# Level totals, query copies and small products of an RWKV time-mix and feed-forward kernel, in another order and form

## The reference

```python
xx  = x_prev - x
mix = tanh((x + xx * time_maa_x) @ maa_w1).reshape(b, t, 5, 32)
mw, mk, mv, mr, mg = einsum('btfe,fec->fbtc', mix, maa_w2)
r, k, v = (x + xx * (maa_r + mr)) @ Wr.T, ...          # one form for each
g = silu((x + xx * (maa_g + mg)) @ Wg.T)
w = time_decay + tanh((x + xx * (maa_w + mw)) @ td_w1) @ td_w2
decay = exp(-exp(w))
# per head of 32 channels, token after token:
y = r @ (S + u * k v^T);   S = decay * S + k v^T
x = layernorm(x + (groupnorm(y) * ln_g + ln_b) * g @ Wo.T)
h = layernorm(gelu(x @ sign(W_fc)^T)) ;  x = layernorm(x + h @ sign(W_proj)^T)
```

## Time and profile before

| what | value |
|---|---|
| median of 3 runs | 3308.46 us (3307.17 to 3309.01) |
| the profiled execution | 3307.6 us |
| its span, first to last instruction | 3305.7 us |
| PE busy | 3080.0 us, 93% |
| DVE busy | 2449.2 us, 74% |
| ACT busy | 1913.6 us, 58% |
| POOL busy | 933.9 us, 28% |
| mean granted TensorE clock | 0.982 |

### The profile page before, as it was taken

One profiled execution on the slowest core, in us unless ns is written; L12 is line 12 of the kernel. 1 busy time (PEld: TensorE's weight loads), 2 busy tenths in 40 slices (PEclk: granted clock), 3 DMA queues, 4 the chain that ended last, 5 costly groups with the idle time before them and its releaser, 6 DMA issues.

```text
span 3305.7 us, 98915 instructions
## 1 busy us (share of the span) xinstructions
PE 3080.0 (93%) x39133; PEld 2229.9 (67%) x39133; DVE 2449.2 (74%) x5172; ACT 1913.6 (58%) x3919; POOL 933.9 (28%) x825
## 2 busy tenths in 40 slices
PE   1899999999999999999999999999999999999997
PEld 0667666767666767666767666767666767666765
DVE  8467787777787777787777687777777777787777
ACT  0456566556566556566655566655566655566654
POOL 3223322223322223322233322233322233322232
PEclk9899999999999999999999999999999999999999
DMA  5000000000000000000000000000000000000000
GB/s 198 14 8 21 15 18 21 18 14 21 15 18 21 18 14 21 16 17 21 18 14 21 20 13 21 18 15 20 21 12 21 18 16 19 21 12 21 18 21 14
DMA packets 22741, 73.24 MB, mean 22 GB/s; under 512 B 3088, under 2 KB 3344, under 8 KB 20688
## 3 DMA queue, kind: packets, MB, share of 16 engines
q1 hardware_dynamic: 22352, 66.96, 5.9%
HBM read 50.17 MB, written 16.78 MB: 20 GB/s over the span
## 4 chain that ended last, share of the span: by engine, by line
PE 48%; DVE 27%; ACT 13%; issue 10%; DVEq 1%; DMA 1%; ACTq 0%; POOL 0%; SPq 0%; POOLq 0%
PE psP L393 10%; PE psP L425 7%; PE psF L637 5%; PE psP L591 5%; ACT HHI L820 4%; PE psF L618 4%; DVE HLO L1288 4%; ACT ARENA L661 3%; DVE ARENA L1138 3%; ACT GG L811 2%; DVE SUMS L1280 2%; DVE ARENA L1126 2%; PE psW L464 2%; PE psW L481 2%; DVE ARENA L1169 2%
## 5 line engine op out<-in xcount | busy, mean ns | idle before, releaser
L661 ACT ACTIVATE ARENA<-ARENA 32x512 f32<-32x512 f32 (+3 forms) x1026 | 581.1, 569 | 263.9 <-DVE ARENA L1114 202.1
L393 PE MATMUL psP<-ARENA,WALL 128*128 128x256 f32 x3072 | 688.0, 380 | 0.2 <-ACT ARENA L694 0.2
L393 PEld LDWEIGHTS psP<-ARENA,WALL 128*128 128x128 f32 x3072 | 574.4, 190 | 73.7 <-issue 0.7
L1288 DVE SCALAR_TENSOR_TENSOR HLO<-GG,FWB,HHI 128x128 f16<-128x128 f32 x1024 | 302.0, 357 | 368.1 <-ACT HHI L820 362.9
L618 PE MATMUL psF<-XHI,WFC 128*128 128x128 f16 x4096 | 487.0, 220 | 2.4 <-DVE ST L1306 2.1
L618 PE MATMUL psF<-XLO,WFC 128*128 128x128 f16 x4096 | 485.7, 219 | 0.0
L618 PEld LDWEIGHTS psF<-XHI,WFC 128*128 128x128 f16 x4096 | 400.4, 99 | 31.5 <-issue 26.3
L881 POOL TENSOR_TENSOR ARENA<-ARENA,XT 128x1024 f32<-128x1024 f32 x128 | 278.2, 2174 | 505.5 <-DVE ARENA L1059 505.5
L618 PEld LDWEIGHTS psF<-XLO,WFC 128*128 128x128 f16 x4096 | 401.4, 98 | 17.6 <-issue 10.3
L637 PE MATMUL psF<-WPJ,HHI 128*128 128x512 f16 x1024 | 405.7, 396 | 4.7 <-ACT GG L811 4.7
L637 PE MATMUL psF<-WPJ,HLO 128*128 128x512 f16 x1024 | 402.3, 393 | 0.0
(11 more groups left out here) (164 smaller groups left out, 5298.9 us busy)
## 6 DMA issues: line engine op xcount, KB each, us to landing
XT<-x_ch SPq DMA_DIRECT2D x33, 520.0 KB, 3.4
ARENA<-x_tok SPq DMA_DIRECT2D x32, 512.0 KB, 4.8
out<-OUT SPq DMA_DIRECT2D x64, 256.0 KB, 3.0
WALL<-w_all SPq DMA_DIRECT2D x5, 1024.0 KB, 15.9
ARENA<-wfc SPq DMA_DIRECT2D x4, 1024.0 KB, 8.0
ARENA<-wpj SPq DMA_DIRECT2D x3, 1024.0 KB, 14.8
GG<-wpj SPq DMA_DIRECT2D x1, 1024.0 KB, 18.8
OUT<-w2a SPq DMA_DIRECT2D x8, 64.0 KB, 15.2
```

Source lines behind the costliest of these rows:

```text
L393: mm = pe.matmul(psP[:, P.bank(f"{name}{g}"), COLS * c:COLS * (c + 1)], WALL[:, w, k, 128 * (2 * g + c):128 * (2 * g + c + 1)], cc(XF[slot ...
L661: return act.activation(o, i, ACT.Copy)
L1288: e = dve.scalar_tensor_tensor(out=HLO[:, k, :], in0=GG[:, u % 2, 0, 128 * m:128 * (m + 1)], scalar=FWB[:, 0, k:k + 1], in1=HHI[:, k, :], ...
```

## The change

**Totals first.** VectorE forms all six totals in one run (`totals`), behind the second quarter's sums and ahead of the u products. Before, each total followed its level's `scale_left`.

**Queries a level ahead.** In step i of the levels, VectorE scales the right halves of the next level first (`scale_right(i + 2, 2 * n)`), then the left halves of the present one, and then makes its own copy of the next level's queries. ScalarE's copies wait for `r_scaled` as before, which now comes a level sooner.

**Small products in parts.** td1 is formed as two sets of 64 rows, each of 128 columns, at output partitions 0 and 64. ScalarE's tanh takes 128x128 instead of 64x256. td2 takes its two halves from partitions 0 and 64 (TD2 is held twice) into the two banks; ScalarE's exponential of it is eight instructions of 128 columns instead of four of 256. w1b is formed as four sets of 32 rows, each of 64 columns, with four tanh instructions instead of one.

**The high parts of the mixing arguments** are rounded as soon as w1a's tanh is there, and GpSimd's `mix_low` waits for the first rounding alone, and for the second at its ninth instruction.

**No folding.** `fold` is gone. `stats` takes SUMS as it is, eight products with one column instead of two. The next `add` that overwrites SUMS waits for `stats`. In the ring F `stats` of p = 1 now stands ahead of the second product, as it does in the order of TensorE.

```diff
-        TD2 = sb("TD2", [DECR, C])[:, :]
+        TD2 = sb("TD2", [128, C])[:, :]
-        TZ = sb("TZ", [DECR, COLS])[:, :]
+        TZ = sb("TZ", [128, 128])[:, :]
...
+                    if name == "w1a":
+                        mm = pe.matmul(ps[:, 0:COLS], W1[:, k, 0:4 * MIXR], cc(XF[1], k), start=(k == 0), stop=(k == KC - 1))
+                    else:
+                        for q in range(4):
+                            mm = pe.matmul(ps[MIXR * q:MIXR * (q + 1), 0:CH], W1[:, k, 4 * MIXR:5 * MIXR],
+                                           cc(XF[1], k)[:, CH * q:CH * (q + 1)], start=(k == 0), stop=(k == KC - 1),
...
-                    mm = pe.matmul(psP[0:DECR, P.bank("td1"), 0:COLS], TD1[:, k, :], cc(XF[1], k),
-                                   start=(k == 0), stop=(k == KC - 1))
+                    for h in range(2):
+                        mm = pe.matmul(psP[DECR * h:DECR * (h + 1), P.bank("td1"), 0:128], TD1[:, k, :], cc(XF[1], k)[:, 128 * h:128 * (h + 1)],
...
+                for c in range(KC):
+                    for h in range(2):
+                        r = slice(DECR * h, DECR * (h + 1))
+                        mm = pe.matmul(psP[:, P.bank(f"td2{h}"), 128 * c:128 * (c + 1)], TD2[r, 128 * c:128 * (c + 1)], TZ[r, :],
...
-                    pe.wait_ge(sums_folded, 2 * (PAIRS * j + p) + 2)
+                    pe.wait_ge(sums_added, 3 * (PAIRS * j + p) + 3)
...
-                        mm = pe.matmul(psF[:, F.bank(f"st_{p}"), i:i + 1], GR[:, i, :], ONES[:, 0:1], start=True, stop=True)
+                        for m in range(4):
+                            mm = pe.matmul(psF[:, F.bank(f"st_{p}"), i:i + 1], SUMS[:, i, 128 * m:128 * (m + 1)], ONES[:, 0:1],
...
-                        e = act.activation(cc(D, k), psP[:, P.bank(f"td2{g}"), COLS * c:COLS * (c + 1)], ACT.Exp,
+                        e = act.activation(cc(D, k)[:, 128 * g:128 * (g + 1)], psP[:, P.bank(f"td2{g}"), 128 * k:128 * (k + 1)], ACT.Exp,
...
+                def totals():
+
+                    for i in range(NPL):
+                        t = TOT[2 ** i].rearrange("p (q two) -> p two q", two=2)
+                        if i:
+                            dve.wait_ge(tot_ready, NPL * it + i)
+                        dve.tensor_tensor(TOT[2 ** (i + 1)], t[:, 0, :], t[:, 1, :], ALU.mult).then_inc(tot_ready, 1)
...
-                    dve.tensor_tensor(TOT[2 * n], tl, tr, ALU.mult).then_inc(tot_ready, 1)
...
+                dve.wait_ge(d_ready, it + 1)
+                totals()
                 dve.wait_ge(p_act, P.read(it, "r1"))
...
                 for i, n in enumerate(LEVELS):
-                    if i:
-                        scale_right(i + 1, n)
+                    scale_right(i + 2, 2 * n)
                     scale_left(i + 1, n)
+                    if i + 2 < NPL - 1:
+                        queries(i + 2, 4 * n)
...
-                    if ffn and n == 2:
-                        ffn.fold(0, 0)
-                scale_right(5, 32)
-                if ffn:
-                    ffn.fold(0, 1)
                 scale_left(5, 32)
...
-                    ffn.fold(1, 0)
-                    ffn.fold(1, 1)
                     ffn.stored()
```

119 lines of the change are left out of this document (61 added, 58 removed).

## The result

The changed kernel takes 3373.35 us (median, 3366.27 to 3380.26), the kernel before beside it 3308.74 us. The ratio is 1.0196, with a 95% interval of 1.0173 to 1.0219: slower by about 2%, where 1% faster was forecast (3275 us). The profiled execution took 3380.26 us, with a span of 3378.5 us and a mean granted clock of 0.977.

The account below looks back on a forecast made before the run. TensorE, busy 93% of the span, was taken as the bound, with l8's wait and slow clock as the loss. Stages of -0.2, -0.95 and 0 gave -1.15 us, taken as -0.95 over 31 tile steps, ends -3 us: 3275 us, range 3225 to 3312.

Parts of the forecast that it names:

- stage A: Output product to k's product, 16.4 us, TensorE busy nearly all the time; predicted change -0.2 us a tile.
- stage B: k's product to the transposes of the keys, holding the levels and l8's wait; predicted change -0.95 us a tile.
- stage C: Transposes of the keys to the output product, bound by a ScalarE and VectorE chain; predicted change 0.
- the wait for k's bank: Stage A: k's product needs td2's first bank read, full only at td2's end; new wait of 0.6 us.
- 0.1 us in the other direction: Stage A: VectorE's two folds gone bring the tokens' normalisation in time for the transposes; -0.1 us becomes -0.2 us.
- the wait 2.16 us: Stage B: l8's level products waiting for ScalarE's copies of the queries; 2.1 us predicted to go.
- the slow clock: Stage B: TensorE partly at 1.2 GHz behind l8's wait; 1.6 us in the tile shown predicted to go.
- The 0.5 us in front of the keys: Stage B: gain predicted where VectorE's second fold had delayed the last left halves.
- the rivals: New waits absent or small 0.15; parts don't overlap 0.13; clock falls before output product 0.10; no gain 0.10.
- The slower one: Stage C's end: clock falls behind a 1.3 us idle before the output product, up to 1.7 us, 3328 us; chance 0.10.

Follow-up runs that it names:

- the hinted kernel: The changed kernel with a branch hint at the head of TensorE's loop, nothing moved: 3307.05 us, ratio 0.9995.
- the parts alone: The kernel before with only td1, td2 and w1b in parts, rounding as before: 3307.67 us, ratio 1.0000.
- the sums alone: The kernel before with no fold on VectorE and stats taking SUMS in eight one-column products instead of two: 3372.17 us, ratio 1.0197.
- the two last variants: Changed kernel with TensorE branch hint, totals a step earlier, left halves first, rounding as before: 3243.20 us; same with the hint on all five engines: 3240.99 us.
- the unrolled kernel: The changed kernel with TensorE's loop unrolled by two, same instructions in the same order: 3349.51 us, ratio 1.0132.

## Why the prediction was wrong

**The step that failed** is one sentence of stage A: "A pause of 0.36 us at the loop's branch is hidden by the longer `stats`." The pause was read as a small stall with a fixed length, behind which any longer work could hide. It was the visible end of some 4 us, of which the second half of the output product hid the rest. The longer `stats` did the opposite: sixteen short records last 1.7 us, TensorE gets through them too late to be ahead of the branch, and the pause becomes 1.84 us (`stats` to the next product 3.54 us, 1.70 us without the branch's cost). No clock fall was priced at this place; it costs 1.7 us a tile (mixing 0.26, td1 0.56, the second product 0.87 us over their times at full clock). Together 3.5 us, of which 0.65 us is no loss, since in the hinted kernel the transposes wait 1.0 us for VectorE, and k's product is spared the 0.35 us for its bank. In the 25 tiles of the hinted kernel that have no pause stage A is 16.18 us, where 16.24 us was before and 16.04 us predicted: without the branch this stage was right within 0.15 us. The hint gave back 66 of the 98 us between forecast and result; most of the rest is stage B.

**A second price stood at nothing** and was wrong in stage C: "GpSimd's earlier `mix_low` lie beside the output product". It did, and it also lay beside VectorE's remainder, which took 0.74 instead of 0.35 us a block. In the changed kernel the sixteen records hid this loss; alone it cost 88 us. What stood behind VectorE (folds, `stats`, the branch) had not been followed.

**td1 and td2.** Sizes right: 1.03 and 1.09 us (0.95 each predicted), the wait for k's bank 0.35 us (0.6). That they gain was wrong: VectorE's tokens come at the same time (15.23 us behind the output product in the hinted kernel's tiles without a pause, 15.30 before), and with the parts alone even later (15.75). The prediction had counted 0.1 us in the other direction. That the two halves overlap was right, and not only for td2, whose halves lie on different rows: td1's are both on all 128 rows and overlap as well.

**Stage B.** Gone: the wait 2.16 us (2.1 predicted), the slow clock 1.3 us as a mean over the tiles (1.6, from one tile). New: l1 0.87 us (0.8), l4 1.05 (0.85), l8 0.56 (0.25), `stats` 0.94 (1.35). The 0.5 us in front of the keys did not come, and k's and the gate's products take 0.1 us more each. Each is small; together they turn -0.95 us into +0.19 us, 35 us over 31 tiles.

**Right:** the levels' waits change from ScalarE to VectorE at l1, l4 and l8; the clock stays up through them (l8 1.03 us in every tile); the output product waits 1.35 us (1.3); w1b's shorter time is worth nothing in stage C (27.11 us with the parts alone, for 27.09); stage C nearly unchanged (its -0.3 us come with the sums alone too, 26.77 us). Of the rivals, none had the branch. The slower one had the right mechanism, a clock that falls behind a short pause, at the wrong place: in front of the output product it did not fall. Two figures of the prediction don't follow from its own rows, without weight for the result: l8 lost 0.9 us to the slow clock (1.93 - 1.03), not 0.8, and its chances add up to 0.74 for faster (0.52, 0.15 and half of 0.13), not 0.79.

## What to carry to other kernels

A short pause of "issue" at a loop's end is what is left uncovered of a branch that takes microseconds. Look at which instruction stands last ahead of the branch, when it is released, and how much long work is queued ahead of it, and announce the branch before anything is put there; unrolling takes away half of the branches, but here it brought a new pause inside the body. When an engine's work is moved to an earlier time, look at every engine that works in that time, also on other data.

## What the runs showed of the hardware

- A taken branch at the end of TensorE's loop: 4.12 to 4.17 us from the release of a waiting two-product instruction to the next product, as means of four kernels (3.84 to 4.61 us in single tiles). With the hint no pause at 25, 28, 26 and 29 of 29 branches (the changed kernel, the two last variants, the kernel before). In the first three, each of the 79 branches without a pause has a transfer of instructions that begins 1.8 to 2.9 us ahead of `stats`, and none of the 8 with a pause has; why it is missing there was not tried. In the changed kernel without the hint 9 of 29 have one so early and pause all the same, so not each of these transfers is TensorE's target.
- GpSimd's subtractions (32x256, fp32r) beside VectorE's blocks of the remainder (128x128, fp16 out), over the whole changed kernel: 0.35 us for most of the 900 blocks with no subtraction beside them, 0.87 us for the 93 that lie beside them for nine tenths of their time, while the subtractions kept their 0.72 us. With VectorE's additions of 128x1024 in fp32 it is the other way round: they kept their time (1.22 and 1.21 us), and the subtraction that starts with them took 1.80 us for 0.72, in all 31 tiles. Here is the one beside the addition at 1693.10 of the section on the result:

```profile
1693.10 1.80 POOL L893 TENSOR_TENSOR MT<-ARENA 32x256 fp32r<-32x256 f32 x1
```

  The Trainium skill ("GPSIMD Engine Reference", section "1. Specifications") says that GpSimd shares its memory interfaces with VectorE, with contention for VectorE's instructions with two inputs from SBUF. Both of these have two such inputs, and the trace agrees for both; it differs which engine is held up.
- The clock falls behind pauses shorter than 2.1 us, and not each time: in the unrolled kernel, with 2.96 to 3.06 us from `stats` to the next product (a pause of 1.3 us over the 1.70 us inside the body), td1 took 1.03 us in three tiles, 1.91 us in four and 1.60 us in one.
- The name behind a wait can be wrong: 24 of 29 pauses at the branch are put down to GpSimd's `mix_low`, and the hint removed them with GpSimd's work unchanged. In the changed kernel the chain of waits follows this name too.
